# Centring by TensorE and a reordered last part of a recurrent mixer with routed experts

## The chip, the cores and the metric

The kernel runs on one core of a Trainium2 chip. The metric is the device time of one execution in microseconds (us), and lower is better. The engines are TensorE (PE, its weight loads PEld), VectorE (DVE), ScalarE (ACT), GpSimd (POOL) and SyncE (SP, which only issues transfers here).

## The reference

The input x has 16 sequences of 256 tokens with 128 channels. Two layers follow one another, each with a layer norm ahead of it, a layer norm behind it and a residual:

```python
it = sigmoid(x @ Wi.T + bi);  rt = sigmoid(x @ Wr.T + br)
at = exp(-8.0 * softplus(cap_lambda) * rt)
gx = sqrt(1.0 - at ** 2) * (it * x)
h  = at * h + gx                      # a scan over the tokens of a sequence
...
scores = sigmoid(x @ gate_w.T)        # 32 experts
_, topk_ids = top_k(scores + e_bias, 4)
a = silu(x @ w1[e]) * (x @ w3[e]) * weight[e];  out = sum over the 4 of a @ w2[e]
...
x = x + layernorm(mixer(layernorm(x)))
x = x + layernorm(experts(layernorm(x)))
```

## The kernel before

There are 32 tiles of 128 tokens. The **mixer** (the first layer, then the norm and the choice of experts of the second) works on groups of 4 tiles, numbered 0 to 7, in a software pipeline that is written out by hand. `step(s)` on each engine holds work of several groups: with a = s+1, b = s, c = s-1, e = s-2, group a is normed and transposed and its gate product for rt is made, group b is gated and scanned (`gate`, `weight_in`, `scan`), group c gets the norm behind the mixer and its residual, and group e the norm ahead of the experts (`inverse_1`, `norm_1`, `turn_1`), the router's logits and the **choice**: `best`, `take_out` and `chosen` find the four experts of each token and give a mask, `positions` (TensorE) and `rows` turn it into places, and `rows_cast` writes the row numbers by which GpSimd scatters each token to its experts' rows in HBM (xs).

The norm behind the mixer of group c runs like this: `turn_h` (TensorE, L1501) transposes the scanned group into a PSUM bank, `stats_h` and `spread_h` (VectorE) take mean and variance from the bank, `std_h` (ScalarE) the root, `inverse_h` and `shift_h` (VectorE) the scale and shift, `norm_h` (ScalarE, four instructions, L472) writes the normed group hn to SBUF, and `add_h` (VectorE, L843) adds it to x. `stats_1` and `spread_1` then take the statistics of the sum.

`keep_on` (L1431) and `keep_on_in` (L1436) are transposes on TensorE whose results nobody reads; they stand ahead of `positions` and `logits`.

`tables(0, ...)` counts, once four groups have been chosen, the rows of each expert and writes the lists (row_of, expert_of) from which SyncE loads blocks of 128 rows. These are the blocks of the first half of the tokens, since the experts run in two halves, and each half first waits for its scatters. The **loop** of a half works in slots, two blocks a slot: TensorE transposes the blocks (L1611), ScalarE copies them (`xbT`, L639), TensorE makes the products with w1 and w3 (L1616), ScalarE takes silu (L642), VectorE multiplies (`act_a`, L1114), TensorE transposes, ScalarE copies (`aT`), TensorE makes the product with w2 (L1648), VectorE copies it (`yb`, L1123), and it is stored. The first 24 slots of the first half are written out; `ahead`, `aside` and `late` put the rest of the mixer into them, such as the choices of groups 6 and 7, the second half's tables (slots 9 to 14), `shares` and `packed_rows(1, 0)` (slots 14 and 15) and, from slot 16, the parts of `weigh`, which compute the experts' weights.

Each engine runs its instructions in the order in which they are written. Semaphores order the engines against one another.

## Time and profile before

| | |
|---|---|
| time, median of 3 runs | 340.8 us (339.17 to 340.84) |
| span of the profiled execution | 340.3 us; its own time is not shown apart from it |
| busy share of the span | PE 83%, PEld 66%, DVE 75%, ACT 64%, POOL 69% |
| mixer, as far as VectorE's last norm of group 7 | to about 114.5 us |
| first product of the loop | 115.04 us |

The span runs from the first instruction to the last, and the median lies 0.5 us above it. Busy shares are means over stages that have different limits. The granted clock of TensorE is given as a share of full speed: 1.0 is 2.4 GHz, 0.5 is 1.2 GHz.

### The profile page before, as it was taken

What the parts mean: (1) busy time and instruction counts of PE and PEld (TensorE: products, weight loads), DVE (VectorE), ACT (ScalarE), POOL (GpSimd) and SP (SyncE); (2) the same over time, 40 slices, a digit from 0 to 9 for tenths busy, and PEclk for the clock granted to TensorE, in tenths of its full rate; (3) what the DMA queues carried; (4) which work ended last, traced back from release to release, by engine and by line L of the source; (5) the groups of instructions that cost most, each with busy time, mean ns of one, the idle gap of its engine ahead of it and who ended that gap; (6) DMA issues with size and microseconds to landing.
All of it is one profiled execution on the core that took longest, in us unless ns stands there. A gap on an engine that the chain in (4) does not pass through costs nothing.

```text
span 340.3 us, 6589 instructions
## 1 busy us (share of the span) xinstructions
PE 281.3 (83%) x1515; PEld 223.4 (66%) x1516; DVE 256.6 (75%) x976; ACT 217.5 (64%) x546; POOL 235.1 (69%) x272
## 2 busy tenths in 40 slices
PE   4575675697585899999997999999999999999950
PEld 2243252553443798889886999889776766899720
DVE  3778689778989577787447989644578987977796
ACT  6938766888773565555553656555588678865752
POOL 4396777777777777777741777777777777777710
PEclk9965679565876599999999999999999999999995
DMA  4999999961111556667746899876521111421232
GB/s 104 323 309 287 281 279 282 305 158 47 52 51 47 149 156 195 190 192 211 214 146 181 232 268 267 239 215 181 156 56 46 48 53 48 130 72 54 64 94 62
DMA packets 84000, 54.81 MB, mean 161 GB/s; under 512 B 8033, under 2 KB 80513, under 8 KB 83969
## 3 DMA queue, kind: packets, MB, share of 16 engines
q1 hardware_dynamic: 57472, 30.85, 33.3%
q0 software_dynamic: 6912, 14.17, 14.1%
q10 hardware_dynamic: 19584, 9.44, 9.8%
q8 instruction: 12, 0.20, 0.2%
q14 instruction: 20, 0.16, 0.1%
HBM read 25.07 MB, written 29.36 MB: 160 GB/s over the span
## 4 chain that ended last, share of the span: by engine, by line
PE 63%; DVE 16%; ACT 11%; issue 5%; DMA 2%; SPq 1%; ACTq 0%; DVEq 0%
PE bank L1616 13%; PE bank L1648 9%; PE bank L1681 7%; PE bank L1692 7%; PE bank L1686 7%; PE bank L1629 5%; PE bank L1611 4%; PE bank L1484 3%; PE bank L1517 3%; DVE st L744 1%; ACT hn L472 1%; ACT L570 1%; ACT L482 1%; ACT xn2T L539 1%; DMA xb<-xs_dram 1%
## 5 line engine op out<-in xcount | busy, mean ns | idle before, releaser
L435 POOL DMA_INDIRECT yk<-ys_dram,row_ys x108 | 106.5, 986 | 42.7 <-issue 26.2
L426 POOL DMA_INDIRECT xs_dram<-xn_all,row_xs x108 | 108.5, 1004 | 36.2 <-issue 32.6
L1616 PE MATMUL bank<-w,xbT 128*128 x288 | 60.4, 333 | 1.3 <-ACT xbT L639 1.2
L1114 DVE TENSOR_TENSOR act_a<-silu,bank 128x192 f32<-128x192 f32 x72 | 25.4, 352 | 29.7 <-ACT silu L642 26.6
L1616 PEld LDWEIGHTS bank<-w,xbT 128*128 128x128 f32 x288 | 46.0, 193 | 2.3 <-issue 2.1
L639 ACT COPY xbT<-bank 128x256 f32<-128x256 f32 x72 | 26.8, 373 | 31.6 <-PE bank L1611 28.6
L1648 PE MATMUL bank<-w2s,aT 96*128 x288 | 45.6, 280 | 0.1
L1648 PEld LDWEIGHTS bank<-w2s,aT 96*128 96x128 f32 x288 | 37.7, 191 | 2.0 <-issue 1.6
L1692 PE MATMUL bank<-at_at,xn_all 128*128 128x384 f32 (+1 forms) x96 | 34.5, 441 | 3.4 <-DVE at_at L1373 3.3
L642 ACT ACTIVATE silu<-bank 128x192 f32<-128x192 f32 x72 | 23.9, 332 | 20.0 <-PE bank L1616 19.1
L1123 DVE COPY yb<-bank 128x256 f32<-128x256 f32 x72 | 30.3, 421 | 7.3 <-PE bank L1648 6.9
L1681 PE MATMUL bank<-xd,w 128*128 128x384 f32 (+1 forms) x96 | 34.2, 438 | 0.0
L1686 PE MATMUL bank<-xd,w 128*128 128x384 f32 (+1 forms) x96 | 33.8, 434 | 0.0
L674 ACT ACTIVATE yk<-yk,wt_all 128x128 f32<-128x128 f32 x96 | 30.4, 391 | 0.4 <-DMA yk<-ys_dram,row_ys 0.4
L1629 PE MATMUL bank<-ident,act_a 128*96 128x128 f32 x144 | 27.9, 275 | 2.9 <-issue 1.5
L646 ACT COPY aT<-bank 96x256 f32<-96x256 f32 x72 | 26.1, 362 | 5.6 <-PE bank L1629 5.5
L1611 PE MATMUL bank<-ident,xb 128*128 128x128 f32 x144 | 28.7, 281 | 0.2 <-DMA xb<-xs_dram 0.2
L1681 PEld LDWEIGHTS bank<-xd,w 128*128 128x128 f32 x96 | 22.9, 252 | 6.2
L1484 PE MATMUL bank<-xnT,wrT 128*128 128x512 f32 x16 | 15.4, 1064 | 13.6 <-ACT xnT L532 13.1
L1686 PEld LDWEIGHTS bank<-xd,w 128*128 128x128 f32 x96 | 22.6, 252 | 4.2 <-issue 2.0
L1692 PEld LDWEIGHTS bank<-at_at,xn_all 128*128 128x128 f32 x96 | 17.5, 189 | 11.4 <-DVE at_at L1373 6.7
L418 POOL TENSOR_SCALAR yk<-x_sb,mv,rstd 128x128 f32<-128x128 f32 x20 | 16.7, 850 | 9.5 <-DVE rstd L817 9.5
(216 smaller groups left out, 531.6 us busy)
## 6 DMA issues: line engine op xcount, KB each, us to landing
xb<-xs_dram SPq DMA_DIRECT2D x144, 64.0 KB
ys_dram<-yb ACTq DMA_DIRECT2D x72, 128.0 KB
xs_dram<-zeros SPq DMA_DIRECT2D x2, 2048.0 KB, 15.1
ys_dram<-zeros SPq DMA_DIRECT2D x1, 2816.0 KB, 13.5
ys_dram<-zeros SPq DMA_DIRECT2D x1, 2560.0 KB, 17.9
x_sb<-in_L_attn_x_dram SPq DMA_DIRECT2D x8, 256.0 KB, 5.2
xs_dram<-xn_all,row_xs POOLq DMA_INDIRECT x108
yk<-ys_dram,row_ys POOLq DMA_INDIRECT x108, 2.5
```

The costliest lines, as they stand in the source:

```text
L426: pool.indirect_dma_start(out=xs[h], out_offset=bass.IndirectOffsetOnAxis(ap=row_xs[:, j, k:k + 1], axis=0), in_=xn2_all[:, j, :], in_offs ...
L435: pool.indirect_dma_start(out=yk[h][:, j - h * TP, k, :], out_offset=None, in_=ys[h], in_offset=bass.IndirectOffsetOnAxis(ap=row_ys[:, j, ...
L639: act.copy(xbT[:, p, :, :].rearrange("c b t -> c (b t)"), ps_xbT[p][:, 0:2 * P]).then_inc(b_xc[h], 1)
L674: ins = act.activation(row, row, ACT.Identity, scale=wt_all[:, g * GT + j, k:k + 1])
L1123: dve.tensor_copy(yb[:, (i + 1) % BODY, :, :].rearrange("t b c -> t (b c)"), ps_y[o][:, 0:2 * P]).then_inc(b_yc[h], 1)
L1611: ins = pe.transpose(ps_xbT[p][:, b * P:(b + 1) * P], xb[:, 2 * i + b, :], ident[:])
L1616: ins = pe.matmul(ps_gu[o][:, b * 2 * I:(b + 1) * 2 * I].rearrange("t (w a i) -> t w a i", w=2, a=1), xbT[:, o, b, :], w13[:, :, bass.ds(e ...
L1629: ins = pe.transpose(ps_aT[p][0:I, b * P:(b + 1) * P], act_a[:, p, b, :], ident[:])
L1648: ins = pe.matmul(ps_y[o][:, b * P:(b + 1) * P], aT[:, o, b, :], w2s[:, bass.ds(expert(i - 3, b), 1), :].rearrange("i a c -> i (a c)"), st ...
L1681: pe.matmul(gates_of(e)[0], w1s[:, at], xd[:, PASS[n]], start=True, stop=True).then_inc(d_gu, 1)
L1686: pe.matmul(gates_of(e)[1], w3s[:, at], xd[:, PASS[n]], start=True, stop=True).then_inc(d_gu, 1)
L1692: pe.matmul(ps_out[n], w2p[:, piece, :], act_e[i][:, here], start=piece == 0, stop=piece == PIECES - 1).then_inc(d_y, 1)
```

## The change

Steps 0 to 4 stay as they are but for a few instructions. Steps 5, 6 and 7 become `dense_step` with another order, and with d = s-2 and e = s-3.

- Groups 4, 5 and 6 are transposed by a product with a matrix `cen`, the unit matrix less 1/128 everywhere, which GpSimd makes at the start. The bank then holds rows with their mean taken off. VectorE still takes their variance (`stats_h`, `spread_h`), and `join_h` multiplies the bank's rows by the scale and adds them to x in one instruction for each tile. `norm_h`, `shift_h` and `add_h` fall away for these groups. Group 7 keeps the old way.
- `std_1`, the root for the second norm, comes a step later.
- The gate products of a group are both made in the step ahead, `gate_i` too.
- The choice of group e comes a step later, so that the loop's slots take the choices of groups 5, 6 and 7. There `rows_cast(6)` and `rows_cast(7)`, `packed_rows(0, ...)`, `shares` and `packed_rows(1, 0)` move by some slots.
- `turn_1` and `logits` of group 6 move into slots 0 and 2 of the loop. `tables(0, ...)` come at other places. The transposes of `keep_on` and `keep_on_in` fall away from group 3 on.

Of the diff, the pieces of ScalarE come first (the first `dense_step` and slot 0's part of `late`), then those of VectorE (`join_h`, `last`, `aside`) and of TensorE (`turn_h` and its own `dense_step`). VectorE's `dense_step` is seen in the rows behind the diff.

```diff
+        DENSE = 5
+        CENTRED = range(DENSE - 1, G - 1)
+            pool.tensor_scalar(cen[:], ident[:], -1.0 / C, None, ALU.add).then_inc(s_const, 1)
...
+            def dense_step(s):
+                a, b, c, d, e = s + 1, s, s - 1, s - 2, s - 3
+                gate_r(b)
+                gate_i(b)
+                if s > DENSE:
+                    score(e)
+                factor(b)
+                act.preload_act_table(ACT.Sqrt)
+                if real(a):
+                    turned_x(a)
+                std_1(d)
+                root(b)
+                std_h(c)
+                turned_1(d)
+                if a + 1 in BY_ACT:
+                    norm_x(a + 1)
+                if real(a):
+                    act.preload_act_table(ACT.Tanh)
...
                 if t == 0:
                     act.preload_act_table(ACT.Silu)
+                    score(G - 3)
+                    turned_1(G - 2)
                     most.append(steps_value(act, 0))
...
+            def join_h(g):
+                dve.wait_ge(v_rstdh, g + 1)
+                for j in range(GT):
+                    dve.scalar_tensor_tensor(out=tile(g * GT + j), in0=ps_h[:, j * P:(j + 1) * P], scalar=rstdh[:, j:j + 1],
+                                             in1=tile(g * GT + j), op0=ALU.mult, op1=ALU.add).then_inc(v_x1, 1)
...
+            def last():   
+                stats_h(G - 1)
+                spread_h(G - 1)
+                stats_1(G - 2)
+                spread_1(G - 2)
+                inverse_h(G - 1)
+                shift_h(G - 1)
                 inverse_1(G - 2)
                 norm_1(G - 2)
...
+                elif t == 5:
+                    rows_cast(G - 3)
                     best(G - 1)
...
+                    if t == 16:
+                        shares()
+                    if t == 18:
+                        packed_rows(1, 0)
...
+                else:
+                    pe.wait_ge(v_x1, GT * g)
+                    if g in CENTRED:
+                        ins = pe.matmul(ps_h[:, j * P:(j + 1) * P], hT[:, j * P:(j + 1) * P], cen[:], start=True, stop=True)
...
+            def dense_step(s):
+                a, b, d, e = s + 1, s, s - 2, s - 3
+                if real(a):
+                    turn_x(a)
+                    gate_r(a)
+                else:
+                    tables(0, 1)
+                if s > DENSE:
+                    positions(e)
+                if s == G - 1:
+                    tables(0, 2)
+                turn_1(d)
+                if real(a):
+                    gate_i(a)
+                logits(d)
+                turn_h(b)
```

VectorE at the start of step 6, before (rstd and xn_all are the second norm of group 4, sth and mvh the statistics of group 5's mixer rows, top_rows and row_xs the cast of group 3, at_at and gated belong to group 6, biased to the choice of group 4):

```order
L868 RECIPROCAL rstd<-std 128x4
L873 TENSOR_SCALAR xn_all<-x_sb,mv,rstd 128x128 x4
L744 BN_STATS sth<-bank 128x6 x4
L749 BN_AGGR mvh<-sth 128x2 x4
L792 MAX top_rows<-val_all 128x8
L795 CAST row_xs<-top_rows 128x4
L886 TENSOR_TENSOR at_at<-at_at 128x512
L880 SCALAR_TENSOR_TENSOR gated<-ti_tr,xnT 128x512
L760 SCALAR_TENSOR_TENSOR biased<-th_all,ebias_half 128x4x32
```

The same place now:

```order
L916 SCALAR_TENSOR_TENSOR gated<-ti_tr,xnT 128x512
L789 SCALAR_TENSOR_TENSOR biased<-th_all,ebias_half 128x4x32
L794 MAX top<-biased 128x8 x4
L773 BN_STATS sth<-bank 128x6 x4
L778 BN_AGGR mvh<-sth 128x2 x4
L922 TENSOR_TENSOR at_at<-at_at 128x512
L801 MATCH_REPLACE left<-top,biased 128x36 x4
L904 RECIPROCAL rstd<-std 128x4
L806 TENSOR_TENSOR mask<-left,biased 128x128
L909 TENSOR_SCALAR xn_all<-x_sb,mv,rstd 128x128 x4
```

The step now opens with the gating of group 6; the second norm of group 4 has moved behind it, and biased and mask are those of group 3, a group later than before.

TensorE in step 5, before (wiT and wrT are the two gate products, xn_all the second norm's transposes, gateT the logits, seen, mask and base the places of the choice, yk the transposes of the next group's normed x, hT the mixer's rows):

```order
L1477 MATMUL bank<-xnT,wiT 128x512
L1508 MATMUL bank<-ident,xn_all 128x128 x4
L1436 MATMUL bank<-ident 128x128 x2
L1517 MATMUL bank<-gateT,xn2T 128x32 x4
L1431 MATMUL bank<-ident 128x128 x8
L1458 MATMUL bank<-seen,ones 128x64
L1461 MATMUL bank<-mask,ones 128x32
L1463 MATMUL bank<-base,ones 128x32
L1464 MATMUL bank<-mask,before 128x32
L1494 MATMUL bank<-ident,yk 128x128 x4
L1484 MATMUL bank<-xnT,wrT 128x512
L1501 MATMUL bank<-ident,hT 128x128 x4
```

TensorE in step 6 now, which places the same group 3:

```order
L1569 MATMUL bank<-ident,yk 128x128 x4
L1559 MATMUL bank<-xnT,wrT 128x512
L1533 MATMUL bank<-seen,ones 128x64
L1536 MATMUL bank<-mask,ones 128x32
L1538 MATMUL bank<-base,ones 128x32
L1539 MATMUL bank<-mask,before 128x32
L1591 MATMUL bank<-ident,xn_all 128x128 x4
L1552 MATMUL bank<-xnT,wiT 128x512
L1600 MATMUL bank<-gateT,xn2T 128x32 x4
L1582 MATMUL bank<-cen,hT 128x128 x4
```

The mixer's rows now come last, behind the next group's second gate product and the logits of group 4, and the transposes on ident alone are gone.

TensorE from the end of step 7 into the first slots of the loop, before (xb is a slot's blocks, w the experts' weights):

```order
L1508 MATMUL bank<-ident,xn_all 128x128 x4
L1436 MATMUL bank<-ident 128x128 x2
L1517 MATMUL bank<-gateT,xn2T 128x32 x4
L273 TENSOR_LOAD steps_of
L273 ISA x2
L1611 MATMUL bank<-ident,xb 128x128 x2
L1625 TENSOR_LOAD expert_of
L1611 MATMUL bank<-ident,xb 128x128 x2
```

The same place now:

```order
L1584 MATMUL bank<-ident,hT 128x128 x4
L279 TENSOR_LOAD steps_of
L279 ISA x2
L1710 MATMUL bank<-ident,xb 128x128 x2
L1591 MATMUL bank<-ident,xn_all 128x128 x4
L1728 TENSOR_LOAD expert_of
L1710 MATMUL bank<-ident,xb 128x128 x2
```

Group 6's transposes and logits stood ahead of the first blocks; now its transposes stand between the first two slots, and its logits in slot 2.

## Rows read from the trace of the kernel before

**Rows 1.** Busy time by stretch: PE, PEld, DVE, ACT, POOL, granted clock, DMA share, GB/s.
```profile
69.90:114.50 44.60, 30.88 (x146) 20.30 (x144) 39.19 (x201) 30.33 (x57) 34.24 (x35) 0.69 0.22 70
...
130.00:140.00 10.00, 10.00 (x75) 8.96 (x74) 8.00 (x42) 5.74 (x18) 7.56 (x9) 1.00 0.65 193
```

**Rows 2.** The chain that ended last, 98 to 128 us (start, length, what).
```profile
105.56 0.88 DVE st L744 x4
...
112.09 1.91 PE bank L1517 x8
```

**Rows 3.** Timeline, VectorE, the choice of group 5 (start, length).
```profile
100.67 0.28 DVE L760 SCALAR_TENSOR_TENSOR biased<-th_all,ebias_half 128x128 f32<-128x128 f32 x1
...
102.49 0.17 DVE L835 RECIPROCAL rstdh<-stdh 128x4 f32<-128x4 f32 x1
...
103.38 0.28 DVE L783 TENSOR_TENSOR val_all<-bank,mask 128x128 f32<-128x128 f32 x1
...
109.94 0.47 DVE L792 MAX8 top_rows<-val_all 128x8 f32<-128x32 f32 x4
```

**Rows 4.** Timeline, VectorE: the add of one group, and nearest pieces for its replacement.
```profile
104.86 0.67 DVE L843 TENSOR_TENSOR x_sb<-x_sb,hn 128x512 f32<-128x512 f32 x1
...
334.89 0.72 DVE L1286 TENSOR_SCALAR hn<-bank,mv,rstd 128x128 f32<-128x128 f32 x2
...
337.21 0.61 DVE L1422 SCALAR_TENSOR_TENSOR x_sb<-yk,rstd,x_sb 128x128 f32<-128x128 f32 x2
```

**Rows 5.** Timeline, VectorE, instructions that waited (in brackets: idle time before, releaser).
```profile
75.10 0.69 DVE L880 SCALAR_TENSOR_TENSOR gated<-ti_tr,xnT 128x512 f32<-128x512 f32 x1 [1.12 <-ACT ti_tr L505]
...
83.37 0.21 DVE L981 TENSOR_SCALAR quot<-bank,round_up 33x1 f32<-33x1 f32 x1 [0.71 <-PE bank L1558]
...
95.29 0.15 DVE L988 COPY upto<-bank 33x1 f32<-33x1 f32 x1 [1.21 <-PE bank L1562]
```

**Rows 6.** Timeline where step 5 begins: VectorE and TensorE.
```profile
68.01 2.05 PE L1484 MATMUL bank<-xnT,wrT 128*128 128x512 f32 x2 [0.77 <-ACT xnT L532]
...
69.53 0.38 DVE L749 BATCH_NORM_AGGREGATE mv<-st 128x2 f32<-128x6 f32 x4
...
69.85 1.06 PE L1501 MATMUL bank<-ident,hT 128*128 128x128 f32 x4
```

**Rows 7.** Timeline: a logits product at full clock, and the first slots of the loop.
```profile
98.90 1.08 PE L1517 MATMUL bank<-gateT,xn2T 128*128 128x32 f32 x8 [0.46 <-ACT xn2T L539]
...
112.83 0.30 ACT L520 ACTIVATE std<-mv,eps_c 128x4 f32<-128x4 f32 x1 [0.79 <-DVE mv L749]
...
114.52 0.37 ACT L639 COPY xbT<-bank 128x256 f32<-128x256 f32 x1 [1.40 <-PE bank L1611]
...
117.76 1.18 PE L1616 MATMUL bank<-w,xbT 128*128 x4
...
119.73 0.59 ACT L539 COPY xn2T<-bank 128x512 f32<-128x512 f32 x1
...
123.80 0.81 PE L1616 MATMUL bank<-w,xbT 128*128 x4
...
147.30 0.81 PE L1616 MATMUL bank<-w,xbT 128*128 x4
...
148.84 0.81 PE L1616 MATMUL bank<-w,xbT 128*128 x4
```

**Rows 8.** Timeline, VectorE, slots 14 to 16 of the loop.
```profile
142.52 0.28 DVE L1006 CAST expert_of<-bank 1x128 int32<-1x128 f32 x1 [0.67 <-PE bank L1648]
...
143.25 0.30 DVE L1134 TENSOR_REDUCE dsum<-comb 128x5 f32<-128x160 f32 x1
...
144.39 0.35 DVE L1114 TENSOR_TENSOR act_a<-silu,bank 128x192 f32<-128x192 f32 x1
```

**Rows 9.** GpSimd: the page's group of its norms, and its scatters by line.
```profile
L418 POOL TENSOR_SCALAR yk<-x_sb,mv,rstd 128x128 f32<-128x128 f32 x20 | 16.7, 850 | 9.5 <-DVE rstd L817 9.5
...
L426 POOL DMA_INDIRECT xs_dram<-xn_all,row_xs x108: 955/962/1460, 34.2 to 174.4; - x108
```

More of the change, by code:

```diff
@@ L259, in routed, with normed @@
             return TH[half(g)] - (GH - 1) * GT if g % GH == GH - 1 else GT
+        def normed(g):
+            return sum(n not in CENTRED for n in range(g))
         def by_act(g):
@@ L566, in step @@
                     norm_x(a + 1)
-                if real(c):
+                if real(c) and a < DENSE:
                     std_1(c)
@@ L614, in _ @@
             second()
-            for s in range(2, G):
+            for s in range(2, DENSE):
                 step(s)
+            for s in range(DENSE, G):
+                dense_step(s)
             last()
@@ L916, in step @@
                     gate(b)
-                if real(e) and e < G - 1:
+                if real(e):
                     best(e)
@@ L925, in step @@
                     weight_in(b)
-                if real(e) and e < G - 1:
+                if real(e):
                     rows(e)
-                    if e + 1 not in LATE:
+                    if s < DENSE - 1:
                         rows_cast(e)
-                    if routed(e) < GT:
-                        scores_of(e)
                 if real(b):
@@ L937, in step @@
                     spread_1(c)
-            def last():
+            def dense_step(s):
+                b, c, d, e = s, s - 1, s - 2, s - 3
+                if s == DENSE:
+                    rows_cast(e)
+                gate(b)
+                if s > DENSE:
+                    best(e)
+                stats_h(c)
+                spread_h(c)
+                square(b)
+                if s == G - 1:
+                    tables(0, 1)
+                if s > DENSE:
+                    take_out(e)
+                inverse_1(d)
+                if s > DENSE:
+                    chosen(e)
+                norm_1(d)
+                weight_in(b)
+                if s > DENSE:
+                    rows(e)
+                    if routed(e) < GT:
+                        scores_of(e)
+                inverse_h(c)
+                if s == G - 1:
+                    tables(0, 2)
+                scan(b)
+                join_h(c)
+                if s < G - 1:
+                    stats_1(c)
+                    if s > DENSE:
+                        rows_cast(e)
+                    spread_1(c)
+                else:
+                    rows_cast(e)
+            def last():
+                stats_h(G - 1)
[4 more added lines that the diff above has]
+                shift_h(G - 1)
                 inverse_1(G - 2)
                 norm_1(G - 2)
-                inverse_h(G - 1)
-                shift_h(G - 1)
-                rows_cast(G - 3)
                 by_tile(G - 1)
@@ L1097, in _ @@
             second()
-            for s in range(2, G):
+            for s in range(2, DENSE):
                 step(s)
-                if s == G - 1:
-                    stats_h(s)
-                    spread_h(s)
-                if s > GH:
-                    tables(0, s - GH - 1)
+            for s in range(DENSE, G):
+                dense_step(s)
+                if s == G - 2:
+                    tables(0, 0)
             last()
@@ L1171, in ahead @@
             def ahead(t):
-                if t in (5, 7):
-                    rows(G - 2 + (t - 5) // 2)
+                if t in (3, 5, 7):
+                    rows(G - 3 + (t - 3) // 2)
                 if t in (9, 11, 13):
@@ L1534, in step, with dense_step @@
                     gate_r(a)
+                if a == DENSE:
+                    gate_i(a)
                 if real(b):
                     turn_h(b)
-            def last():
-                turn_1(G - 2)
-                logits(G - 2)
+            def dense_step(s):
+                a, b, d, e = s + 1, s, s - 2, s - 3
+                if real(a):
+                    turn_x(a)
+                    gate_r(a)
+                else:
+                    tables(0, 1)
+                if s > DENSE:
+                    positions(e)
+                if s == G - 1:
+                    tables(0, 2)
+                turn_1(d)
+                if real(a):
+                    gate_i(a)
+                logits(d)
+                turn_h(b)
             def second():
@@ L1576, in _ @@
             second()
-            for s in range(2, G):
+            for s in range(2, DENSE):
                 step(s)
-                if s > GH:
-                    tables(0, s - GH - 1)
-            last()
+            for s in range(DENSE, G):
+                dense_step(s)
+                if s == G - 2:
+                    tables(0, 0)
             def ahead(t):
-                if t in (5, 7):
-                    positions(G - 2 + (t - 5) // 2)
+                if t in (3, 5, 7):
+                    positions(G - 3 + (t - 3) // 2)
                 if t in (9, 11, 13):
@@ L1619, in slot @@
                     ins.then_inc(b_gu[h], 1)
+                if h == 0 and isinstance(t, int) and t == 0:
+                    turn_1(G - 2)
                 if h == 0 and isinstance(t, int) and t == 1:
                     turn_1(G - 1)
+                if h == 0 and isinstance(t, int) and t == 2:
+                    logits(G - 2)
                 if h == 0 and isinstance(t, int) and t == 3:
```

55 lines of the change are left out of this document (28 added, 27 removed).

## The prediction

> **What bounds the kernel now.** I first read busy time by stretch. From the end of step 4's statistics (69.9 us) to the last norm of group 7 (114.5 us) VectorE is busy 39.19 of 44.60 us; TensorE has 30.88, ScalarE 30.33 and a mean granted clock of 0.69 [rows 1]. In the loop TensorE has 10.00 of 10.00 us at clock 1.0, with VectorE at 8.00 [rows 1]. The chain of waits says the same: from 98 us it is VectorE's pieces one after another, with ScalarE's norm between, until TensorE's logits of group 6 at 112.09 [rows 2]. So before the loop an edit is worth what it takes off VectorE's work and waits; in the loop it is worth what it takes off TensorE's time, and TensorE follows VectorE and ScalarE there in places. Past slot 23 nothing is touched, so I count how much earlier or later that slot comes, and carry it to the end unchanged.
>
> The durations come from one execution with a span of 340.3 us; the median run is 340.8, and I add the sum to that. A difference of 0.5% (1.7 us) is about what a measurement of this kernel can tell from none.
>
> **VectorE's work before the loop.** The choice of group 5 leaves it: 1.82 us from 100.67 to 102.49, then 0.28 for its places and 0.47 for its row numbers [rows 3], with about 0.1 for the two short instructions behind those: -2.7. Groups 4 to 6 lose `add_h`, 0.67 each [rows 4], and the short `shift_h` (0.1 by my estimate): -2.3. They gain `join_h`, an operation on four 128-wide tiles that reads PSUM, SBUF and a scale per row. The trace has it in no place. The nearest rows are the same operation from SBUF, 0.61 for two, and a scaling from PSUM, 0.72 for two [rows 4]; four therefore cost 1.1 (if they overlap better in a longer run) to 1.45, and I take 1.2, as the operation itself is that of the first row: +3.6 for three (3.3 to 4.35). In all -1.4 (-1.7 to -0.65).
>
> The Trainium skill (VectorE: DVE Perf Modes, the section on the TRN2 errata) says that each instruction pays a fixed cost and that small tiles pay it once per tile, which speaks against four tiles in place of one 512-wide add. Its figures would make four reads from PSUM 1.03 us as an estimate, and the three joins 0.5 us cheaper than I take them. No join has run here, and the measured neighbours decide.
>
> **VectorE's waits before the loop.** Three that it has now go, as what they waited for is moved: 1.12 for gate i, 0.71 and 1.21 for the tables [rows 5]; -3.0. New ones come. (a) Step 5 opens with `gate(5)`, which needs both gate products. TensorE starts the first at 68.01 and its next work at 69.85 [rows 6], so at that half clock a product takes 1.84 and the second ends at 71.7; ScalarE's tanh behind it takes about 0.6, as a 512-wide copy does [rows 7]. VectorE is free at 69.91 [rows 6] plus 0.55 for the row numbers of group 2 (0.47 [rows 3] and the short one). It waits 1.8 (1.0 if the second product ran at full clock). Everything of the step is queued behind it. (b) `turn_h(4)` now stands behind that product, and centring needs four full products. The floor is four transposes, 1.06 [rows 6]; the nearest kind are four logits products in eight pieces, 1.08 at full clock [rows 7], up to 2.16 at half. I take 1.9; they end at 73.6, `gate(5)` at 73.0: 0.6 (0 to 0.9). (c) In step 6 `gate(6)` opens again and needs ScalarE's whole round first, which ends with a table load and two gates: 0.6 (0 to 1.1, the present wait for that gate). (d) The first table stays a wait behind a step's last product: 0.4 (0 to 0.7). (e) `turn_h(7)` must wait until `join_h(6)` has read the bank, and stands behind the logits of group 5; now VectorE has an add and two statistics to do meanwhile: 0.7 (0 to 1.1). Sum +4.1 (1.0 to 5.6), with the 3.0 gone +1.1 (-2.0 to +2.6).
>
> The last root before the loop, which ends at 113.13 [rows 7], thus comes 0.3 earlier.
>
> **The loop's first slots.** Behind that root ScalarE copies the first blocks, and now waits 1.40 for TensorE [rows 7], which has the logits of group 6 in the way. They move into slot 2, and the blocks should be there, as the tables are ready in step 7: -1.4 (-1.4 to -0.9). The scatters must be done too: they start at 34.2 and 108 take until 174.4 [rows 9], 1.31 each, so the 52 of the first half are issued by 102. Group 3's four, whose row numbers come about six microseconds later than now, at some 92, are due only at 97; were that cover gone, the blocks would come later one for one.
>
> Added to slots 0 to 4: the logits of group 6, 1.08 at full and 2.16 at half clock [rows 7], 1.5; the places of group 5, at most that, 0.4; on ScalarE a 512-wide copy, 0.59 [rows 7], ahead of slot 1's blocks, 0.6; and the products start earlier on a clock that is low there now (slot 2 takes 1.18 where slot 5 takes 0.81 [rows 7]), 0.5. But slots 2 to 5 now take 6.04 us where an undisturbed slot takes 1.54 [rows 7], so 1.4 of waiting is there to be filled, and I take half: -0.7. `turn_1(6)` lies in TensorE's wait for the first copies. Sum +2.3 (0.6 to 4.0). Slot 5 comes at -0.3 - 1.4 + 2.3 = +0.6.
>
> **Slots 5 to 23.** Slot 5 gets one more `best`, about 0.8 (0.28 [rows 3] and the four maxima, which cost what those of the row numbers do). VectorE has a fifth of a slot free [rows 1], 0.3: +0.5 (0 to 0.8). `shares` takes 1.14, from 143.25 to 144.39 [rows 8], in slot 14, where VectorE has just waited 0.67 for TensorE; that covers half of it. In slots 16 and 18 it and `packed_rows(1, 0)`, some 0.6, stand beside a part of `weigh` each, without that cover: 1.7 of work against 0.3 free in each of three slots leaves 0.8, of which the two buffers catch some: +0.5 (0 to 1.7).
>
> GpSimd makes `cen` in one 128-wide instruction, 0.85 by its neighbours, where it idles 9.5 for VectorE [rows 9]: nothing, and 0.85 at the first norms if that were gone. The scatters of the second half end a few microseconds later, long before their half begins.
>
> **Sum:** 0.6 + 0.5 + 0.5 = +1.6, so 342.4.
>
> **Rivals.** *The clock stays up.* TensorE gets the centring products and loses gaps, and if it is granted 1.0 throughout, (a) falls by 0.8, (b) by 0.6, (d) and (e) by 0.4, the slots' logits by 0.4 and their first products by 0.5: 339.7. For it: in the loop, where TensorE is never idle, the clock is 1.0 [rows 1]. Against: TensorE still waits in each step for masks and norms. The Trainium skill (TensorE: Matmul & The Clock Gate, Part 1) says that the engine is throttled unless it is active; by that rule a denser TensorE ends here if the gaps are short enough. The two stretches agree with its direction, 0.69 at 30.88 of 44.60 busy and 1.0 at full.
>
> *VectorE no longer waits in steps 5 to 7.* ScalarE sheds twelve norms and gets ahead; then (a) to (e) vanish, -4.1: 338.3, faster. It decides on `gate_i(5)`: it must be over when VectorE is free at 70.5. Against it stands the product that ran at half clock just before [rows 6].
>
> *The clock comes later in the loop.* The idle transposes are gone, and TensorE waits before slot 1. Each further slot at half clock costs up to 1.54 more, as slot 2 shows in part; two such slots make 345.5, slower.
>
> **How the numbers follow.** The forecast case gets 0.61, with its own range 340.5 to 344.3: about 0.33 lies within 1.7 us of no change and 0.28 above. The clock that stays up gets 0.14 (0.03 faster, 0.11 same), VectorE without waits 0.12 (faster), the late clock 0.13 (slower). That makes 0.15 faster, 0.44 the same and 0.41 slower. The range leaves out the fastest rival and half of the late clock: 339.4 to 344.8.
>
> **What would show it.** In the changed kernel's timeline: four joins in about 1.2; `gate(5)` waiting near 1.8; the last root of the mixer within a microsecond of 112.8; the first product of the loop some 1.7 earlier than 115.04; slot 5 near 124.4; and slots 16 to 19 longer than 1.54. I am wrong if the root comes 2 us or more earlier (the waits were not new), if slots 2 to 5 are no longer than now (the moved choices were free), or if the clock is low beyond slot 4.

## The result, and the profile after

The changed kernel takes 343.56 us in the median of its runs (341.09 to 346.58), the kernel before 341.53 beside it (339.17 to 342.66). The ratio is 1.0054, 95% interval 1.0038 to 1.0071: slower by 0.54%, some 1.8 us. The forecast was 342.4 in a range of 339.4 to 344.8. Every run lists its time and its span, and they lie about 1.8 us apart. The profiled execution shown first has a span of 344.8 and took 346.58: it is the longest of the twenty and stays out of the ratio. A second profile of the same kernel, with a span of 342.0 and the median's time, stands below as the twelfth run.

**The mixer** ends nearly when it was forecast to end. By stretch (columns as in [rows 1]) and by group of instructions (xcount, busy us, mean ns of one, idle us before them and what ended it):

```profile
69.90:114.50 44.60, 27.49 (x115) 19.57 (x113) 36.71 (x186) 26.13 (x47) 33.73 (x34) 0.61 0.26 78
```
```profile
L773 DVE BATCH_NORM_STATS2 sth<-bank 128x6 f32<-128x128 f32 x16 | 3.5, 284 | 1.5 <-PE bank L1584 1.2 <-PE bank L1582 0.3
L879 DVE SCALAR_TENSOR_TENSOR x_sb<-bank,rstdh,x_sb 128x128 f32<-128x128 f32 x12 | 3.3, 332 | 0.0
L916 DVE SCALAR_TENSOR_TENSOR gated<-ti_tr,xnT 128x512 f32<-128x512 f32 x3 | 2.1, 691 | 3.3 <-ACT ti_tr L512 3.3
```

Against [rows 1] VectorE is busy 2.5 us less in this stretch, and TensorE 3.4. The joins (L879) take 332 ns a tile in the mean. The new waits are there: 3.3 us in sum for the gates' tanh (L512) and 1.5 for the mixed rows' statistics. The mean granted clock fell from 0.69 to 0.61. The first product of the loop, before and after:

```profile
115.04 1.64 PE L1616 MATMUL bank<-w,xbT 128*128 x4
```
```profile
113.25 1.49 PE L1715 MATMUL bank<-w,xbT 128*128 x4
```

**The loop of the first half** gives that back. A slot is counted here from its first product with w1 and w3 to the next slot's; the loop's first product opens slot 1. These are TensorE's instructions that waited in slots 3, 5 and 7 (start, length; in brackets the idle time before and what ended it), and behind them the same instructions before:

```profile
119.23 1.05 PE L1600 MATMUL bank<-gateT,xn2T 128*128 128x32 f32 x8 [0.60 <-ACT xn2T L546]
...
124.53 0.23 PE L1533 MATMUL bank<-seen,ones 128*128 128x160 f16 x1 [0.55 <-DVE mask L806]
...
129.30 0.20 PE L1533 MATMUL bank<-seen,ones 128*128 128x96 f16 x1 [0.98 <-DVE mask L806]
```
```profile
120.47 1.05 PE L1517 MATMUL bank<-gateT,xn2T 128*128 128x32 f32 x8 [0.44 <-ACT xn2T L539]
...
124.67 0.23 PE L1458 MATMUL bank<-seen,ones 128*128 128x160 f16 x1
...
128.79 0.20 PE L1458 MATMUL bank<-seen,ones 128*128 128x96 f16 x1 [0.50 <-ACT aT L646]
```

L1533 (before: L1458) is the first product of `positions`. In slots 5 and 7 it now waits for the mask of group 6 and of group 7, which VectorE has only just made. So slot 5 lasts 2.64 us (1.92 before), slot 7 3.07 (2.43) and slot 3 3.60 (3.04). By slot 16 the loop is 0.47 behind the kernel before, and the last product of the first half starts at 178.42, before at 177.94.

**The half change** takes most of what is then lost. In the program SyncE waits for all of the second half's scatters before it loads that half's blocks. GpSimd's waits for row numbers (us in all, times, longest), before and after, and its scatters after, in order of time:

```profile
POOL xs_dram L426 <- DVE row_xs L795: 3.6, 1, 3.6
```
```profile
POOL xs_dram L433 <- DVE row_xs L824: 6.4, 3, 3.6
```
```profile
105.19 0.95 POOL L433 DMA_INDIRECT xs_dram<-xn_all,row_xs  x1 [1.11 <-DVE row_xs L824]
...
127.15 0.96 POOL L433 DMA_INDIRECT xs_dram<-xn_all,row_xs  x1 [1.70 <-DVE row_xs L824]
...
177.12 0.96 POOL L433 DMA_INDIRECT xs_dram<-xn_all,row_xs  x1 [0.31 <-issue]
```

Before, GpSimd waits once for row numbers, 3.6 us ahead of the first scatter. Now it also waits 1.11 for those of group 4 and 1.70 for those of group 5, and the last scatter goes out at 177.12 instead of 174.36 [rows 9]. TensorE feels it. Its timeline at the half change and the stretches behind it, after:

```profile
182.95 0.33 PE L1710 MATMUL bank<-ident,xb 128*128 128x128 f32 x1 [1.02 <-DMA xb<-xs_dram]
183.56 0.46 PE L1710 MATMUL bank<-ident,xb 128*128 128x128 f32 x1 [0.28 <-DMA xb<-xs_dram]
184.37 0.48 PE L1710 MATMUL bank<-ident,xb 128*128 128x128 f32 x1 [0.36 <-DMA xb<-xs_dram]
184.64 1.49 PE L1715 MATMUL bank<-w,xbT 128*128 x4
```
```profile
180.00:182.00 2.00, 1.81 (x11) 1.35 (x11) 1.09 (x3) 0.37 (x1) 0.00 (x0) 1.00 0.45 127
...
184.00:186.00 2.00, 1.64 (x7) 1.46 (x6) 1.62 (x7) 0.37 (x1) 0.00 (x0) 0.50 0.58 157
186.00:188.00 2.00, 2.00 (x9) 1.75 (x8) 0.74 (x5) 0.78 (x3) 0.75 (x1) 0.50 0.47 130
```

And before:

```profile
177.94 0.82 PE L1616 MATMUL bank<-w,xbT 128*128 x4
...
181.08 0.79 PE L1611 MATMUL bank<-ident,xb 128*128 128x128 f32 x4
182.81 0.91 PE L1616 MATMUL bank<-w,xbT 128*128 x4 [0.94 <-ACT xbT L639]
```
```profile
184.00:186.00 2.00, 1.01 (x8) 0.71 (x8) 1.88 (x11) 0.72 (x3) 0.61 (x1) 1.00 0.47 129
```

TensorE now waits for three of the four first blocks, the clock falls to 0.50, and the second half's first product starts at 184.64 and takes 1.49. Before, it starts at 182.81 and takes 0.91. How long the clock stays low varies: in this profile it is 0.50 from 184 to 190, in the twelfth run's only from 184 to 186.

### The profile page after: what moved, and what is told of

The parts are those of the page before. It is cut to its first block, busy times and chain, and to the rows that moved or that the text cites. A ratio compares the mean times of both kernels' runs of the same rounds, so it can differ in the third digit from the quotient of the medians.

```text
span 344.8 us, 6544 instructions
## 1 busy us (share of the span) xinstructions
PE 281.1 (82%) x1495; PEld 224.3 (65%) x1496; DVE 256.6 (74%) x982; ACT 212.9 (62%) x534; POOL 235.1 (68%) x273
## 4 chain that ended last, share of the span: by engine, by line
PE 49%; DVE 13%; ACT 12%; POOL 11%; issue 8%; DMA 4%; SPq 2%; POOLq 0%; ACTq 0%; DVEq 0%
POOL xs_dram L433 11%; PE bank L1784 7%; PE bank L1795 7%; PE bank L1789 7%; PE bank L1715 6%; PE bank L1751 4%; PE bank L1559 3%; PE bank L1600 3%; DMA xb<-xs_dram 2%; PE bank L1710 2%; PE bank L1732 2%; PE bank L1552 1%; ACT xn2T L546 1%; DVE st L773 1%; SPq L333 1%
## 5 line engine op out<-in xcount | busy, mean ns | idle before, releaser
L442 POOL DMA_INDIRECT yk<-ys_dram,row_ys x108 | 105.3, 975 | 41.8 <-issue 27.1
L1715 PE MATMUL bank<-w,xbT 128*128 x288 | 61.7, 339 | 0.0
L1715 PEld LDWEIGHTS bank<-w,xbT 128*128 128x128 f32 x288 | 47.1, 197 | 0.1
L1710 PE MATMUL bank<-ident,xb 128*128 128x128 f32 x144 | 30.4, 288 | 7.5 <-issue 5.4
L1559 PE MATMUL bank<-xnT,wrT 128*128 128x512 f32 x16 | 14.5, 1002 | 15.8 <-ACT xnT L539 15.4
L1710 PEld LDWEIGHTS bank<-ident,xb 128*128 128x128 f32 x144 | 18.8, 147 | 10.3 <-issue 6.1
```

The lines of the kernel that those rows point to most:

```text
L442: pool.indirect_dma_start(out=yk[h][:, j - h * TP, k, :], out_offset=None, in_=ys[h], in_offset=bass.IndirectOffsetOnAxis(ap=row_ys[:, j, ...
L1710: ins = pe.transpose(ps_xbT[p][:, b * P:(b + 1) * P], xb[:, 2 * i + b, :], ident[:])
L1715: ins = pe.matmul(ps_gu[o][:, b * 2 * I:(b + 1) * 2 * I].rearrange("t (w a i) -> t w a i", w=2, a=1), xbT[:, o, b, :], w13[:, :, bass.ds(e ...
```

## The experiments

Four times of an execution tell nearly all of what follows: **F**, the start of the loop's first product; **E**, of the last product of the first half; **Q**, of the last scatter; **S**, of the first product of the second half. This table is read from the timelines of all fourteen profiles; "37-40" is the time from S to the second half's fourth product. The kernel before was timed beside each group of runs and had medians of 341.2 to 341.6, so times of different groups compare to about 0.4.

```
                           F      E   E-F       Q       S   S-E    S-Q  37-40   span
before                115.04 177.94 62.90  174.36  182.81  4.87   8.45  4.84  340.3
before, again (8)     111.81 174.26 62.45  174.60  181.27  7.01   6.67  4.88  339.5
before, late (4)      114.75 177.34 62.59  176.90  183.97  6.63   7.07  5.09  342.0
before, short (5)     114.16 175.87 61.71  162.93  180.76  4.89  17.83  4.83  338.9
after                 113.25 178.42 65.17  177.12  184.64  6.22   7.52  6.26  344.8
after, again (12)     112.61 177.58 64.97  176.67  183.69  6.11   7.02  5.12  342.0
after, group 4 (1)    111.33 175.82 64.49  175.13  182.15  6.33   7.02  4.88  340.0
after, group 5 (2)    111.62 176.41 64.79  174.30  181.70  5.29   7.40  5.27  340.1
after, both (3)       112.67 177.91 65.24  174.06  182.79  4.88   8.73  4.83  341.3
after, short (6)      113.62 178.37 64.75  167.28  183.33  4.96  16.05  4.83  341.6
after, uncentred (7)  113.32 178.05 64.73  177.53  186.33  8.28   8.80  5.80  345.8
spread, early (9)     113.08 175.97 62.89  175.03  182.00  6.03   6.97  7.57  343.0
spread, late (10)     110.36 173.06 62.70  175.14  182.11  9.05   6.97  4.64  341.0
spread, short (11)    114.71 176.94 62.23  165.43  181.92  4.98  16.49  4.83  340.8
```

My first theory was the queue alone: the late row numbers of groups 4 and 5 end the scatters later, and that is the loss. Its rival was the work added to the loop's slots.

**1 to 3: the row numbers earlier.** Run 1 makes those of group 4 ahead of the joins of step 7, run 2 those of group 5 a slot earlier, run 3 both.

```diff
                 scan(b)
+                if s == G - 1:
+                    rows_cast(e)
                 join_h(c)
...
-                else:
-                    rows_cast(e)
```
```diff
                 elif t == 4:
+                    rows_cast(G - 3)
                     take_out(G - 2)
                     chosen(G - 2)
                 elif t == 5:
-                    rows_cast(G - 3)
                     best(G - 1)
```

> The changed kernel with one edit: in step 7 the row numbers of group 4 are made ahead of the three joins instead of behind them. Theory (the second half starts when GpSimd's queue of scatters has run out, and the changed kernel leaves that queue idle for 1.11 us at group 4 and 1.70 us at group 5): the wait at 105 us goes, but the queue then stands 1.1 us longer at group 5, whose row numbers still come at 127; the last scatter stays at 177.1 and the time within 0.7 us of the changed kernel, 343 to 344. Rival A (the loss is extra work in the loop's slots and the new products): no change either. Rival B (every delay of the mixer counts by itself): 1.1 us slower or faster, as the joins shift.

Measured: 343.71, ratio to before 1.0072 (1.0046 to 1.0098), as long as the changed kernel. Q comes 63.80 behind F, after the change alone 63.87: the queue only waits longer at group 5 (2.75), as expected. Rival A expects the same time, so this run does not choose between the two.

> The changed kernel with one edit: the row numbers of group 5 are made in slot 4 instead of slot 5 of the loop. Theory (scatter queue): the wait of 1.70 us at group 5 goes, the one of 1.11 at group 4 stays; the last scatter is issued 1.7 us earlier, near 175.4, the first blocks of the second half are loaded as much earlier, and the time is 1 to 2 us below the changed kernel, 341.5 to 342.5. Rival A (extra work in the slots): the same work stands one slot earlier, no change, 343.5.

Measured: 342.36, ratio 1.0032 (1.0009 to 1.0055). Q is at 174.30, earlier than the theory asked, and GpSimd waits for row numbers only once, 3.2 us ahead of the first scatter. F was early in this profile, so the wait of 1.11 at group 4, which was expected to stay, is gone too. Q-F is 62.68, 1.2 less than after the change alone. The time lies 1.2 below the changed kernel's 343.56, and the two intervals overlap.

> The changed kernel with both edits: the row numbers of group 4 ahead of the joins of step 7 and those of group 5 in slot 4. Theory (scatter queue): GpSimd waits once for row numbers, as before the change, the last scatter is issued near 174.4, TensorE has its first blocks of the second half without a wait and at clock 1.0, and the time is that of the kernel before plus at most the 0.3 us by which slot 24 comes later: 341 to 342. Rival A (extra work in the slots, centring): still 343 to 344.

Measured: 342.54, ratio 1.0041 (1.0019 to 1.0063). Q is back at 174.06 and TensorE has its blocks: GpSimd's waits, and TensorE at the half change:

```profile
POOL xs_dram L433 <- DVE row_xs L824: 4.2, 3, 3.6
```
```profile
181.06 0.87 PE L1710 MATMUL bank<-ident,xb 128*128 128x128 f32 x4
182.79 0.91 PE L1715 MATMUL bank<-w,xbT 128*128 x4 [0.86 <-ACT xbT L668]
```

The first product of the half waits for ScalarE's copy as it does before, at full clock. But the time is 1 us below the changed kernel, not 2: above the expected 341 to 342. The intervals of runs 2 and 3 overlap that of the changed kernel, so the gain of 1 is likely and not shown. Run 3 is still slower than the kernel before (1.0019 at the least): something is left.

**4: one late pair, put into the kernel before.** Only the row numbers of group 5 move from the end of the mixer into slot 5.

```diff
                 shift_h(G - 1)
-                rows_cast(G - 3)
...
                 elif t == 5:
+                    rows_cast(G - 3)
                     rows_cast(G - 2)
```

> The kernel before with one edit: the row numbers of group 5 are not made before the loop but in its slot 5, with those of group 6. Nothing else of the change is in it. Theory (scatter queue): the scatters of group 5 were issued from 125.0 and now wait until about 127, the queue ends 2 us later and the time rises by 1.5 to 3 us, to 343 to 344.5: the size of the whole loss, from this one shift. Rival A (extra work): 0.5 us of work stands in a slot instead of before the loop, 341 to 342, within 0.5 us of the kernel before.

Measured: 343.56, ratio 1.0078 (1.0050 to 1.0106), 2.3 us slower than the 341.24 beside it. GpSimd's waits for row numbers:

```profile
POOL xs_dram L426 <- DVE row_xs L795: 7.7, 2, 4.1
```

Besides the 3.6 ahead of the first scatter there is now a wait of 4.1, at group 5. Q is at 176.90, 2.3 to 2.5 later than in the two profiles of the kernel before, and S 7.07 behind it. E-F is 62.59, as before. One instruction pair of 0.65 us, moved, costs as much as the whole change. The wait is longer here than the 1.70 in the changed kernel, so this run shows the cause and not its size there.

**5 and 6: the queue out of the way.** In both kernels group 7's eight scatters are left out.

```diff
+            for n in range(1, 5):
+                sp.dma_start(xs[1][0:E * REGION, :].rearrange("(e r) c -> r e c", r=REGION)[n * P:(n + 1) * P, :, :],
+                             zeros[:].unsqueeze(1).to_broadcast([P, E, C])).then_inc(s_pad[1], 16)
...
-                sp.wait_ge(s_scat[h], 16 * TH[h] * K)
+                sp.wait_ge(s_scat[h], 16 * (TH[h] - h * routed(G - 1)) * K)
...
-            for g in range(G):
+            for g in range(G - 1):
+                if g == GH:
+                    pool.wait_ge(s_pad[1], 112)
                 scatter(g)
```

> The kernel before with a shorter queue of scatters: the eight scatters of group 7 are left out (its rows stay zero: the second half's first 512 rows of each expert are filled with zeros early on, so that the blocks hold numbers). The queue ends 10 us earlier, near 164, so the second half can start as soon as the first half is over. Theory (in the kernel before, the end of the first half decides, 4.87 us before the second half's first product): little or nothing is gained, 0 to 1.3 us. It is the base for the next run; the zero fill may cost something in both alike. Rival (what remains of the loss is in the loop or behind it): the same here.

> The changed kernel with the same shorter queue, group 7's scatters left out and the same zero fill; the late row numbers of groups 4 and 5 stay late. Theory (scatter queue): with the queue out of the way the end of the first half decides in both kernels, and that comes 0.5 us earlier in the mean of the four profiles of the changed kernel and its variants than in the two of the kernel before; the time is that of the short kernel before, -1.0 to +0.5 us. Rival A (the loss is extra work in the loop's slots and the centring): 2 us above the short kernel before, as with the full queue. Rival B (half of it is queue, half is something behind the half change): about 1.2 us above.

Measured: 341.09 and 344.06, ratios 0.9976 (0.9952 to 0.9999) and 1.0072 (1.0050 to 1.0094). The difference is 3.0 us where the queue decides nothing. Here the theory of the queue alone falls, and its rival A stands. TensorE's first products of the second half, short before and short after:

```profile
180.76 0.91 PE L1621 MATMUL bank<-w,xbT 128*128 x4 [0.96 <-ACT xbT L644]
```
```profile
183.33 0.91 PE L1720 MATMUL bank<-w,xbT 128*128 x4 [0.97 <-ACT xbT L673]
```

S is 4.89 and 4.96 behind E, at full clock in both, and E lies 2.5 apart: F came 0.54 earlier, but slots 1 to 36 take 64.75 us for 61.71. From S to the end the two take the same, 158.2. I had expected E half a microsecond earlier, from the few profiles that I had then; but F alone varies by 3 to 4 us among profiles of one order of the mixer (111.81 to 115.04 with the old one, 110.36 to 114.71 with the new), and E with it.

**7: without the centring.**

```diff
-        CENTRED = range(DENSE - 1, G - 1)
+        CENTRED = range(G, G)
...
                 std_h(c)
+                norm_h(c)
...
                 inverse_h(c)
+                shift_h(c)
...
-                join_h(c)
+                add_h(c)
```

> The changed kernel with one part undone: TensorE transposes the mixed rows of groups 4 to 6 again, ScalarE norms them and VectorE adds them in one 512-wide add behind a short shift, in place of the centring products and the joins; the order of the steps stays. Theory (scatter queue): the mixer moves by a microsecond or so, and what counts is when VectorE has the row numbers of groups 4 and 5; the time is within 1 us of the changed kernel, 342.5 to 344.5. Rival A (centring and joins are the loss): back to 341.5 to 342. By the prediction's sum the joins cost VectorE 1.3 us more than the two instructions they replace, while ScalarE is spared twelve norms: the last root of the mixer moves by 1.3 earlier to 2 later.

Measured: 347.58, ratio 1.0168 (1.0125 to 1.0211), 4 us above the changed kernel and outside what either theory gave. F and E are those of the changed kernel; Q is 0.4 to 0.9 later. S is 8.80 behind Q, since the blocks land late:

```profile
183.85 0.33 PE L1712 MATMUL bank<-ident,xb 128*128 128x128 f32 x1 [2.40 <-DMA xb<-xs_dram]
184.42 0.47 PE L1712 MATMUL bank<-ident,xb 128*128 128x128 f32 x1 [0.24 <-DMA xb<-xs_dram]
185.74 0.80 PE L1712 MATMUL bank<-ident,xb 128*128 128x128 f32 x2 [0.84 <-DMA xb<-xs_dram]
186.33 1.49 PE L1717 MATMUL bank<-w,xbT 128*128 x4
```

Centring is not the loss: undone in the new order, the kernel is slower. What centring is worth by itself this does not show, since F and E are the same and the time goes at the half change. The delay there is in the loads: SyncE issues the first 2.9 behind Q, as elsewhere (2.6 to 2.9), but TensorE has that block 3.5 us later, in run 8 2.0. Why they land later I have not found.

**8 and 12: both kernels once more.**

> The kernel before once more, for a second profile of it: how far its first product of the loop, the end of its first half and the start of its second vary from one execution to the next. Theory (scatter queue): last scatter within 0.3 us of 174.4, and a second half that starts 4.9 us after the last product of the first or 7.1 us after the last scatter, whichever is later.

Measured: 341.36. TensorE at the half change:

```profile
174.26 0.82 PE L1616 MATMUL bank<-w,xbT 128*128 x4
...
179.12 0.33 PE L1611 MATMUL bank<-ident,xb 128*128 128x128 f32 x1 [1.54 <-DMA xb<-xs_dram]
179.87 0.33 PE L1611 MATMUL bank<-ident,xb 128*128 128x128 f32 x1 [0.42 <-DMA xb<-xs_dram]
180.72 0.76 PE L1611 MATMUL bank<-ident,xb 128*128 128x128 f32 x2 [0.52 <-DMA xb<-xs_dram]
181.27 1.49 PE L1616 MATMUL bank<-w,xbT 128*128 x4
```

This changed my picture of the kernel before. Here F comes 3.2 us earlier than in the profile that the prediction was read from, the first half ends 3.7 earlier, and S comes only 1.5 earlier: TensorE now waits for blocks, because the last scatter goes out at 174.60, no earlier than the 174.36 of the first profile.

> The changed kernel once more, for a second profile of it. Theory (in the changed kernel both limits of the second half hang on the loop's first product, F): the row numbers of group 5 come 13.9 us after F, the last scatter is issued 63.9 after F, the first half's last product starts 64.5 to 65.2 after F, and the second half's first product about 71 after F, a microsecond and more behind what the end of the first half alone would allow (4.9 behind its last product). Rival (the scatters end by the clock of GpSimd alone, and the first profile was an odd one): last scatter at 177.1 whatever F is. Time 343 to 344.

Measured: 343.75, ratio 1.0050 (1.0007 to 1.0092). GpSimd's waits and last scatter:

```profile
104.56 0.95 POOL L433 DMA_INDIRECT xs_dram<-xn_all,row_xs  x1 [1.11 <-DVE row_xs L824]
...
126.59 0.95 POOL L433 DMA_INDIRECT xs_dram<-xn_all,row_xs  x1 [1.78 <-DVE row_xs L824]
...
176.67 0.96 POOL L433 DMA_INDIRECT xs_dram<-xn_all,row_xs  x1 [0.31 <-issue]
```

Q is 64.06 behind F, E 64.97 and S 71.08, each as expected. In these two profiles of the changed kernel Q moves with F, since the row numbers of group 5 are made in slot 5.

**9 to 11: the choices spread over more slots.** With two causes on the table, these take the slots' part away: groups 6 and 7 are chosen in slots 4 to 9, with two slots between a mask and the places counted from it. Run 9 has early row numbers like run 3 (those of group 5 in slot 3), run 10 the late ones, run 11 is run 9 with the short queue. The second half's tables move from slots 9 to 14 into 13 to 18, and the row numbers of groups 6 and 7 into slots 7 and 11. The core of the edit, in `aside` and in both `ahead`:

```diff
-                elif t == 3:
-                    best(G - 2)
                 elif t == 4:
-                    take_out(G - 2)
-                    chosen(G - 2)
+                    best(G - 2)
                 elif t == 5:
-                    best(G - 1)
-                elif t == 6:
+                    take_out(G - 2)
+                    chosen(G - 2)
+                elif t == 8:
+                    best(G - 1)
+                elif t == 9:
                     take_out(G - 1)
                     chosen(G - 1)
...
-                if t in (3, 5, 7):
-                    positions(G - 3 + (t - 3) // 2)
+                if t in (3, 7, 11):
+                    positions(G - 3 + (t - 3) // 4)
```

> The changed kernel with both early casts of the third experiment (row numbers of group 4 ahead of the joins, those of group 5 in slot 3), and the choices of groups 6 and 7 spread over slots 4 to 11 instead of 3 to 9, with two slots between a mask and the places that TensorE counts from it; the second half's tables come in slots 13 to 18 instead of 9 to 14. Theory (two causes: the slots with a choice are longer by 2.5 us in sum, and the late row numbers end the scatters 1 to 3 us later): TensorE no longer waits for masks, slots 1 to 36 take 63.0 to 63.8 us instead of 64.8 (62.4 in the kernel before), the queue ends near 174.3, and the time is 1 to 1.5 below the 342.5 of the third experiment, 341.0 to 341.6: that of the kernel before. Rival A (what remained in the third experiment lies behind the half change): 342.5, as there. Rival B (the work only moves to other full slots): slots 1 to 36 stay at 64.8 and the time at 342.5.

Measured: 343.66, ratio 1.0058 (1.0033 to 1.0082): a miss in the time. The slots did what was expected, 62.89 for 65.24: slot 5 lasts 1.53, slot 7 1.93. But the second half starts 6.97 behind the last scatter, which at 175.03 is 1.0 later than in run 3, and the clock falls. No late row number holds the queue there: at groups 4 to 7 GpSimd waits 0.3 at the most, and its 108 scatters themselves take 109.1 us, in run 3 108.1. TensorE there, and the stretch:

```profile
180.42 0.33 PE L1711 MATMUL bank<-ident,xb 128*128 128x128 f32 x1 [0.62 <-DMA xb<-xs_dram]
181.22 0.33 PE L1711 MATMUL bank<-ident,xb 128*128 128x128 f32 x1 [0.47 <-DMA xb<-xs_dram]
181.84 0.33 PE L1711 MATMUL bank<-ident,xb 128*128 128x128 f32 x1 [0.30 <-DMA xb<-xs_dram]
182.00 0.85 PE L1716 MATMUL bank<-w,xbT 128*128 x4
...
184.44 1.49 PE L1716 MATMUL bank<-w,xbT 128*128 x4
```
```profile
184.00:186.00 2.00, 1.88 (x8) 1.70 (x8) 0.05 (x1) 0.40 (x2) 0.98 (x1) 0.50 0.45 127
186.00:188.00 2.00, 2.00 (x9) 1.88 (x8) 1.33 (x6) 1.04 (x3) 1.43 (x2) 0.50 0.46 112
188.00:190.00 2.00, 2.00 (x11) 1.99 (x10) 0.97 (x5) 0.89 (x3) 1.42 (x2) 0.53 0.73 160
```

S to the fourth product takes 7.57 instead of the 4.83 of run 3: the 2 us that the slots gave are gone by slot 40.

> The changed kernel with the spread choices of groups 6 and 7 alone; the row numbers of group 4 stay behind the joins and those of group 5 in slot 5. Theory (two causes): slots 1 to 36 shorten as in the run before, but the scatters still end near 176 to 177 and the second half cannot start before about 7 us behind that; of the 1 to 1.5 us little or nothing is got, 342.8 to 343.6. Rival A (the slots alone): 1 to 1.5 below the changed kernel, 342.0 to 342.6. Rival B (neither): 343.5.

Measured: 343.41, ratio 1.0060 (1.0034 to 1.0086), the time that the theory gave. E is the earliest of all, 173.06, and S is still 182.11, because Q is at 175.14. But the theory's reason is not in this profile. GpSimd's waits for row numbers:

```profile
POOL xs_dram L433 <- DVE row_xs L824: 3.3, 1, 3.3
```

F is so early, at 110.36, that the row numbers of groups 4 and 5 are in time: the only wait stands ahead of the first scatter. What holds S is the queue itself. In the six profiles with all scatters and no such wait above 0.3 us behind the first (both of before, runs 2, 3, 9 and 10) Q is at 174.06 to 175.14, and S comes at 181.27 at the earliest, however early E is.

> The kernel of the ninth experiment with the shorter queue of the fifth and sixth: group 7's scatters are left out and its rows stay zero, with the same zero fill. With the queue out of the way, the loop's slots are all that is left between the two kernels. Theory (two causes): slots 1 to 36 decide; 1 to 1.5 us below the short changed kernel (344.1), 342.5 to 343.0, and at most 2 us above the short kernel before (341.1). Rival A (behind the half change): 344, as the short changed kernel.

Measured: 342.39, ratio 1.0034 (1.0008 to 1.0060), just under the expected 342.5 to 343.0. Without the queue's limit the spread choices are worth 1.7 us against run 6, and 1.3 remain to the short kernel before. Here slots 1 to 36 take 62.23 against 64.75.

So the slots' part pays only where the queue is out of the way. Of the versions that do all the work none beats the kernel before; run 2 comes nearest.

## Why the prediction was right, and where not

The sign and the size of the time were right; that the sum came out is in good part luck. It carried +1.6 from slot 24 to the end. In the profiled pair the last product of the first half comes only 0.48 later, and the rest comes of a wait that the sum put at nothing. By its own steps:

- **The base.** The profile of before has a span of 340.3, so its execution took 342.1, and I set the median's 340.8 beside it as if they were one. Its F of 115.04 is the latest of the four profiles with the old mixer (111.81 to 115.04). Half of the argument spoke of a stretch that varies by 3 us from one execution to the next, and of which the kernel before passes on only a part, as run 8 shows.
- **VectorE's work, -1.4.** The joins took 1.09 to 1.10 for four where I took 1.2. The Trainium skill's figures (VectorE: DVE Perf Modes, the TRN2 errata) made 1.03 of it as an estimate; the traces lie between, nearer to the Trainium skill's. From 69.90 to the end of the last root VectorE is busy 35.32 us for 37.90: 2.6 less. Of the 1.2 beyond the forecast the cheaper joins are 0.3.
- **The waits, +1.1.** All five came: (a) 1.98 for 1.8, (b) 0.29 for 0.6, (c) 1.29 for 0.6, (d) 1.05 and 0.44 for 0.4, (e) 1.25 for 0.7. That is 6.3 in sum where I had 4.1. In all VectorE idles 7.45 us up to the root's end, before 5.33: 2.1 more, forecast 1.1. The two misses, in work and in waits, cancel, and the last root ends at 112.67, forecast 112.8.
- **The first product** starts 1.79 earlier than in [rows 7]'s execution, forecast 1.7. Over the profiles with the old mixer's order (four) and with the new centred one (nine) the means are 113.9 and 112.6: 1.4 earlier, less than either group spreads (3.2 and 4.4), so the gain is likely and not shown.
- **Slots 0 to 4, +2.3.** Mis-sized: from F to slot 5 it is 9.70 for 8.76, +0.9. Slot 2, which now holds the logits of group 6 (0.97), is only 0.46 longer. And the clock, from which I added 0.5, rose earlier: it is 0.98 from 115.04 to 117.00, and slot 2's product takes 0.82, before 1.18.
- **Slots 5 to 23, +1.0.** From slot 5 to slot 10 it is 10.63 for 9.27, +1.4 where I had +0.5: I counted VectorE's extra work against its free time, and the cost was TensorE's wait for two masks, each made only in the slot ahead of its use. From slot 10 to 16 nothing changed. From slot 16 to 24 it is 12.97 in run 8 and 13.42 in run 12, +0.45, forecast +0.5; in the first two profiles it is 13.50 and 13.30, so this one is not settled.
- **"Past slot 23 nothing is touched ... carry it to the end unchanged", and the scatters of the second half that end "long before their half begins".** This is the step that failed. With all scatters in the queue the second half begins at 181 to 186, 6.7 to 8.8 us behind its last scatter. S follows E by 4.9 or Q by 7, whichever is later, to 0.5 us in thirteen of the fourteen profiles. In the kernel before both lie close together and either can decide; the late row numbers pushed Q 2.1 to 2.8 later. I read the first half's scatters against their due time and not the second half's, though [rows 9] gave 174.4.

So +1.8 comes of this. The loop's first half takes 2.3 to 2.5 more (E-F 62.45 and 62.90 before, 64.97 and 65.17 after), and runs 5, 6 and 11 show what that is worth where the queue decides nothing. The mixer probably gives some of it back. The row numbers of groups 4 and 5 put the second half's start on the queue: run 4 shows the cause by itself, and run 3 gets back 1.0 in overlapping intervals. The parts do not add up singly, since S takes the later of two. Between the profiles of runs 8 and 12, whose times are close to their medians, S moves by 2.4 and the stretch behind it not at all (158.3 in both).

What stays open is the stretch from S to the end, 157.5 to 161.0 us among the profiles. The last 100.1 us of it, from the first product of slot 72, are the same in all fourteen; what varies are slots 37 to 40 (4.64 to 7.57) and 41 to 71 (50.8 to 52.4). Why a late start of the half costs 4.88 there in run 8 and 7.57 in run 9 no run shows, and with it why run 9 is no faster than the changed kernel; the loads of run 7 stay open too.

Of the rivals, the clock did not stay up (0.61, less than before), and VectorE waits more. The late clock came, but at the half change, and not in the loop's first slots. No run puts the idle transposes back, so whether the lower clock in the mixer is due to them is not shown.

## What to carry to other kernels

When a stage starts on the later of two chains, read both ends in the profile, and how far apart they lie, before pricing an edit on one of them: here 2 us won in the slots were worth nothing in the time while the queue of scatters stood, and 1.7 without it. A short instruction that feeds a long queue in order (a cast of 0.65 us ahead of sixteen scatters of 1.26) has its due time from that queue, not from the loop in which it finds room. And one profile of a kernel shows one execution: a stage that varies by 3 us is worth a second look before terms of 0.5 are summed in it.

## What the runs showed of the hardware

- In the five profiles in which TensorE waits for no block at the half change, the clock stayed at 1.00 through it, and slots 37 to 40 take 4.83 or 4.84. In the nine in which it waits for blocks the granted clock fell around the half's first slots, in eight of them to 0.50 over 2 us and more (run 2: a mean of 0.55), and slots 37 to 40 took 4.64 to 7.57. The Trainium skill (TensorE: Matmul & The Clock Gate, Part 1) says that the engine is throttled unless it is active; these rows agree with its direction. They also show that a wait can cost again behind its end: in run 9 the clock is at 0.50 to 0.53 from 184 to 190, well behind the last wait at 181.84.
- Slots 5 to 10 of the loop repeat to 0.05 us from one execution to the next (10.63 to 10.67 us in all seven profiles with the changed order of the choices; slot 5: 2.64 in five of them), while the mixer ahead varies by 3 us and slots 16 to 24 of the kernel before by 0.5 (12.97 and 13.50). Such slot times are the safer rows to compare.
- The product with `cen`, four tiles of 128 columns, took 1.91 us where step 5 begins, at clock 0.50, and 1.16 where step 6 begins, at 1.00; I had taken 1.9, and the transposes that it replaces took 1.06 at 0.50 [rows 6].
